# A fused attention and expert kernel: identity matmuls ahead of the first weights, x rows 2 and 3 loaded third, three jobs from VectorE to ScalarE

## The reference

```
xn = layernorm(x)                                   # over the 128 features
s  = attention(xn)          # blocks, top 64 tokens, windows of 32; gated; layernorm
q  = xn @ Wq.T              # 2 halves x 8 heads x 64
sim = einsum(q, keys)       # 32 keys for each half and head
sx, ix = top_k(sim[0], 16);  sy, iy = top_k(sim[1], 16)
scores, idx = top_k(sx[:, None] + sy[None, :], 16)
f  = sum over the 16 of  gelu(xn . W_down[idx]) * softmax(scores) * W_up[idx]
out = x + s * silu(f)
```

## Time and profile before

| what | value |
|---|---|
| runs of the kernel | 288.28, 289.41 and 291.24 us, median 289.41 us |
| profiled execution, span from first to last instruction | 288.0 us (no other time of this execution is given) |
| mean granted TensorE clock | 0.981 |
| busy share of the span: PE, DVE, ACT, POOL | 84%, 93%, 83%, 79% |
| chain that ended last: DVE, PE, issue, ACT, DMA | 77%, 8%, 6%, 4%, 2% |

### The profile page before, as it was taken

How to read it: one execution, slowest core, us unless ns; L and a number is a source line. 1 busy time by engine, 2 the same in 40 slices (tenths; PEclk the granted TensorE clock), 3 DMA queues, 4 the chain that set the end, 5 groups by cost and what they waited for, 6 DMA issues and landing times.

```text
span 288.0 us, 7869 instructions
## 1 busy us (share of the span) xinstructions
PE 241.3 (84%) x1504; PEld 170.5 (59%) x1504; DVE 267.8 (93%) x2574; ACT 238.1 (83%) x1071; POOL 228.8 (79%) x351
## 2 busy tenths in 40 slices
PE   0789997887989798979897989798979897988792
PEld 0624343474757675767575757575757575756592
DVE  6689999999999999999999999999999999997474
ACT  3338668589898999899989998999899989997832
POOL 8986710378688879997999799979997999798791
PEclk9999999799999999999999999999999999999959
DMA  8920000000000000100010001000100010001002
GB/s 173 272 67 1 3 1 0 0 3 0 2 3 0 2 3 0 39 3 1 1 41 0 3 1 38 5 0 2 38 2 2 3 36 2 5 0 38 3 1 71
DMA packets 11234, 6.27 MB, mean 22 GB/s; under 512 B 1457, under 2 KB 10674, under 8 KB 11186
## 3 DMA queue, kind: packets, MB, share of 16 engines
q1 hardware_dynamic: 9858, 5.12, 6.7%
q10 hardware_dynamic: 1328, 0.66, 1.2%
HBM read 3.67 MB, written 2.10 MB: 20 GB/s over the span
## 4 chain that ended last, share of the span: by engine, by line
DVE 77%; PE 8%; issue 6%; ACT 4%; DMA 2%; SPq 1%; DVEq 0%
DVE rest L1124 27%; DVE top L1113 15%; DVE top L1133 15%; DVE last L1157 7%; DVE slot_gap L1142 2%; DMA x_sb<-in_L_attn_hidden_states 2%; DVE sel_m L1176 2%; DVE st L1048 2%; PE scratch L1550 1%; ACT prob L808 1%; DVE slot_gap L1148 1%; DVE sel_b L1179 1%; DVE sel_a L1179 1%; PE c_bank L1523 1%; DVE mv L1052 1%
## 5 line engine op out<-in xcount | busy, mean ns | idle before, releaser
L1124 DVE MATCH_REPLACE8 rest<-top,sim 128x32 f32<-128x32 f32 x512 | 85.8, 180 | 0.0
L1133 DVE MAX8 top<-rest 128x8 f32<-128x32 f32 x512 | 53.5, 177 | 0.7
L808 ACT ACTIVATE prob<-drop 128x50 f32<-128x50 f32 x232 | 53.4, 255 | 0.0
L1113 DVE MAX8 top<-sim 128x8 f32<-128x32 f32 x496 | 51.1, 183 | 2.2 <-PE sim L1459 2.2
L808 ACT ACTIVATION_READ_ACCUMULATOR prob<-drop 128x1 f32 x232 | 48.7, 213 | 0.0
L488 POOL TENSOR_TENSOR squareT<-sideT 100x512 bf16<-100x512 bf16 x31 | 32.2, 1039 | 14.6 <-ACT sideT L723 14.6
L1124 DVE MATCH_VALUE_LOAD rest<-top,sim 128x8 f32 x512 | 41.1, 80 | 0.3
L1459 PE MATMUL sim<-sim_w,xT_all 128*128 128x512 f32 x64 | 35.2, 633 | 0.9 <-DVE sim_w L1090 0.9
L473 POOL TENSOR_TENSOR past<-gap,last 128x400 f32<-128x400 f32 x31 | 26.7, 862 | 11.4 <-DVE last L1157 11.3
L495 POOL TENSOR_TENSOR drop<-gap,out_by 128x400 f32<-128x400 f32 x31 | 32.0, 1033 | 2.8 <-ACT out_by L714 2.8
L1477 PE MATMUL t_bank<-gaps_of,topT 128*128 128x200 f32 x128 | 29.7, 354 | 2.4 <-ACT topT L728 2.3
(11 more groups left out here) (277 smaller groups left out, 720.0 us busy)
## 6 DMA issues: line engine op xcount, KB each, us to landing
out<-y_sb SPq DMA_DIRECT2D x7, 256.0 KB, 2.3
x_sb<-in_L_attn_hidden_states SPq DMA_DIRECT2D x2, 256.0 KB, 3.9
fwq_sb<-in_L_ffn_Wq ACTq DMA_DIRECT2D x2, 256.0 KB, 5.8
x_sb<-in_L_attn_hidden_states SPq DMA_DIRECT2D x1, 512.0 KB, 5.9
wc_sb<-in_L_attn_Wc SPq DMA_DIRECT2D x1, 256.0 KB
out<-last_y SPq DMA_DIRECT2D x2, 128.0 KB, 1.8
wo_in<-in_L_attn_Wo SPq DMA_DIRECT2D x1, 192.0 KB
keys_sb<-in_L_ffn_keys ACTq DMA_DIRECT2D x1, 128.0 KB, 3.4
```

Source lines behind the costliest of these rows:

```text
L808: last = nc.scalar.activation(prob[d][:, h, :], drop[:, h, :], ACT.Exp, scale=-1.0, accum_out=den[d][:, h:h + 1])
L1113: last = nc.vector.max(top[d][:, v, 0:8], sim_bank[d][:, bass.ts(v, KEYS)])
L1124: last = nc.vector.match_replace(out=rest[:, v, :], in_to_replace=top[d][:, v, 0:8], in_values=sim_bank[d][:, bass.ts(v, KEYS)], imm_value ...
L1133: last = nc.vector.max(top[n % 2][:, v, 8:16], rest[:, v, :])
```

## The change

ScalarE takes over the copy of the transposed keys (ahead of its expert selection copies), the normalisation of row 0 and the copy of the folded weights (both ahead of its loop over the rows). Rows 2 and 3 of x are loaded ahead of the six small loads. TensorE multiplies the identity by 112 of its own columns, 6 times ahead of the key transposes and 8 times behind them, into columns of a PSUM bank that nothing reads. GpSimd waits for row 0 ahead of normalising row 2, as both raise the same semaphore.

```diff
--- before.py
+++ after.py
@@ -298,8 +298,8 @@
         NORM_GROUPS = [(0, 1), (1, 2), (2, 4), (4, 6), (6, B)]
 
         POOL_NORMS = [1, 2, 4, 6]
-        ACT_NORMS = [3, 5, 7]
-        assert sorted([0] + POOL_NORMS + ACT_NORMS) == list(range(B))
+        ACT_NORMS = [0, 3, 5, 7]
+        assert sorted(POOL_NORMS + ACT_NORMS) == list(range(B))
 
 
 
@@ -338,12 +338,12 @@
 
             load_x(0)
             load_x(1)
+            load_x(2)
             sp.dma_start(zw_sb[:, 0:1], ws[:, :]).then_inc(zw_in, 16)
             sp.dma_start(zw_sb[:, 1:4], wg[:, :]).then_inc(zw_in, 16)
             for k, src in enumerate([bs[0:1], bg[0:1], bg[1:2], bg[2:3]]):
                 sp.dma_start(bz_sb[k * B:(k + 1) * B, :],
                              src.rearrange("(a n) -> a n", a=1).to_broadcast([B, 1])).then_inc(zw_in, 16)
-            load_x(2)
             load_x(3)
             for dst, src in ((down_sb, ffn_down), (wup_sb, ffn_up)):
                 sp.dma_start(dst[:, :, :], src[0:2 * P, :].rearrange("(k p) d -> p k d", p=P)).then_inc(down_in, 16)
@@ -447,6 +447,8 @@
                 pool.wait_ge(norm1_ready, g + 1)
                 for b in range(b0, b1):
                     if b in POOL_NORMS:
+                        if b == 2:
+                            pool.wait_ge(xn_done[0], 1)
                         for t in range(TB * b, TB * b + TB):
                             last = nc.gpsimd.tensor_scalar(xn_all[:, t, :], x_sb[:, t, :], rstd1[:, t:t + 1],
                                                            nmr1[:, t:t + 1], ALU.mult, ALU.add)
@@ -688,6 +690,13 @@
                                                 bias=nmr1[:, t:t + 1], scale=rstd1[:, t:t + 1])
                 last.then_inc(xn_done[b % 2], 1)
 
+            act.wait_ge(consts, 3)
+            act.wait_ge(keysT_ready, 1)
+            for half in range(2):
+                c = slice(half * DKEY, (half + 1) * DKEY)
+                last = nc.scalar.activation(keysT[c, :, half, :], f_bank[c, 0:HK].rearrange("p (h k) -> p h k", k=KEYS),
+                                            ACT.Copy)
+            last.then_inc(keysT_out, 1)
             act.wait_ge(consts, CONSTS)
             for at, length, i, j, di, dj in pair_runs(HALF_V):
                 chosen = bass.AP(ident, (i * TOPK + j) % P, [[P, P], [0, 2], [di * TOPK + dj, length]])
@@ -752,6 +761,9 @@
                     last = nc.scalar.activation(wo_sb[:, r, :], wo_in[:, r, :], ACT.Identity, bias=wo_mean[:, r:r + 1])
                 last.then_inc(wo_step, 1)
 
+            norm_rows(0)
+            act.wait_ge(fold_ready, 1)
+            nc.scalar.activation(sim_w[:, :], sim_bank[1][:, :], ACT.Copy).then_inc(sim_w_done, 1)
             for b in range(B):
                 act.wait_ge(xt_full, b + 1)
                 nc.scalar.activation(xT_all[:, bass.ts(b, L)], scratch[b % 2][:, :], ACT.Copy).then_inc(xt_out, 1)
@@ -1069,25 +1081,12 @@
             row_stats(0)
             dve.wait_ge(x_in[1], 16)
             row_stats(1)
-            dve.wait_ge(consts, 3)
-            dve.wait_ge(keysT_ready, 1)
-            for half in range(2):
-                c = slice(half * DKEY, (half + 1) * DKEY)
-                last = nc.vector.tensor_copy(keysT[c, :, half, :], f_bank[c, 0:HK].rearrange("p (h k) -> p h k", k=KEYS))
-            last.then_inc(keysT_out, 1)
-            dve.wait_ge(norm1_ready, 1)
-            for t in range(TB):
-                last = nc.vector.tensor_scalar(xn_all[:, t, :], x_sb[:, t, :], rstd1[:, t:t + 1],
-                                               nmr1[:, t:t + 1], ALU.mult, ALU.add)
-            last.then_inc(xn_done[0], 1)
             dve.wait_ge(gaps_step, 2)
             nc.vector.tensor_tensor(gaps_of[:, :, :], rank_first[:, :].unsqueeze(2).to_broadcast([P, HALF_H, CANDS]),
                                     rank_sum[:, :, :], ALU.subtract).then_inc(gaps_of_done, 1)
             dve.wait_ge(x_in[2], 16)
             row_stats(2)
             row_stats(3)
-            dve.wait_ge(fold_ready, 1)
-            nc.vector.tensor_copy(sim_w[:, :], sim_bank[1][:, :]).then_inc(sim_w_done, 1)
 
             def invert_sums(n):
 
@@ -1407,6 +1406,11 @@
         def _(pe):
             mm = nc.tensor.matmul
 
+            def keep_clock(count):
+
+                for _ in range(count):
+                    mm(t_bank[:, HEADS * CANDS:512], ident[:, :], ident[:, 0:512 - HEADS * CANDS], start=True, stop=True)
+
             def transpose_keys():
 
                 pe.wait_ge(keys_in, 16)
@@ -1738,7 +1742,9 @@
                 last.then_inc(gate_ready, 1)
 
             pe.wait_ge(consts, 2)
+            keep_clock(6)
             transpose_keys()
+            keep_clock(8)
             fold_weights()
             transpose_rows(0)
             pe.wait_ge(xt_out, 1)
```

## The result

The changed kernel took 292.24 us (median of 4 runs, 291.18 to 293.84) against 289.52 for the kernel before. The ratio is 1.0097, with a 95% interval of 1.0055 to 1.0138. A second comparison, with 12 runs, gave 291.95 against 288.87: 1.0090 (1.0057 to 1.0124). It is about 1% **slower**, and outside the range that I gave (287.2 to 291.0). The profiled execution took 291.63 us and has a span of 289.1 us, 1.1 above that of before. The ratios are taken over executions within 1.5% of the fastest of the same kernel, the medians over all.

A forecast was written before the change was run, and what follows sets the result against it. DVE, busy 93%, was taken to bound the kernel; of its 2.7 us lead 0.3 survives, so the span goes from 288.0 to 287.7 and, with the median 1.4 above it, the forecast is 289.1 us, range 287.2 to 291.0.

The forecast's parts named there:

- Where DVE's lead goes: At tile 0's pair gaps: of DVE's 2.7 us lead, 2.3 is waited away; the run gains 0.2 to 0.4 us.
- Step 4: Loads at the start: rows 2 and 3 of x, loaded third, delay the folded weights 0 to 2.9 us; 0.5 taken.
- Step 3: TensorE's start: 28 added identity passes delay the key transposes 0.35 us and end at 7.2 to 8.0 us if fast.
- the sum: Start to DVE's first MAX8 at the fast price: fold from 8.7, scores to 13.0 instead of 15.70, lead 2.7 us.
- Rival B: TensorE's start: lower clock, added passes delay the fold; MAX8 17.0, run 290.7, or 292.4 with fold at 11.1; chance 0.12.
- Rival C: On the path: one half-speed TensorE stretch more or less, 1.6 us, giving 287.5 or 290.7; chance 0.14.
- Steps 2 and 5: ScalarE takes DVE's three jobs, row 0 done at 10.0 us; GpSimd's added wait ahead of row 2; both cost nothing.
- second chain: GpSimd to 20.24 us, then TensorE and ScalarE to the first gap copy's end at 31.20, 0.4 us behind DVE.

## Why the prediction was wrong

**Where DVE's lead goes: right.** I said that a lead at MAX8 is waited away at the pair gaps, whose copy hangs on GpSimd's row 2, and that any MAX8 up to 15.3 us gives the same there. Pair gaps were taken at 31.08 both with MAX8 at 13.06 and at 14.93, with a wait of 2.0 us in the first case. The changed kernel never got there: its MAX8 started at 16.84 to 18.52.

**Step 4, the load order: mis-sized.** I took 0.5 us between bounds of 0 and 2.9. The fold came 2.3 to 2.9 us later in the four profiles, 2.7 with the load order alone: nearly the whole of the upper end. My reason for the lower end, that the small transfers had used the stretch anyway, was wrong. The six of them carry some 2 KB together; what they took was SyncE's time to issue them, from 1.82 to 4.39 us, and the load of x was issued only then, at 4.43. In the changed kernel its issue is the third of these and over by 2.32:

```profile
0.79 1.53 SPq L337 DMA_DIRECT2D x_sb<-in_L_attn_hidden_states  x3
```

So 512 KB entered while the weights, issued from 1.33 us on, were on their way. From 5 to 8 us the windows show 183 to 225 GB/s before and 187 to 286 after: the queues moved no less, and still the weights came later.

**Step 3 and the sum: the step that failed.** I set fold, transposes and scores at the fast price because the passes precede them, and let the passes end at 7.2 to 8.0 and the fold begin at 8.7. I did not ask what the clock does when TensorE has nothing to do between these. With the fold at 10.55 it fell, and the sum ended at 16.84 instead of 13.0. The late weights alone would have left MAX8 near 14.9, as in the profile with the clock held, within the 15.3 up to which I said that steps 3 and 4 need not be sized well. With the fall of the clock it went past that bound. Had I carried the upper bound of step 4 through, I would have seen a wait of over 3 us behind the passes. Nothing in the rows of before shows what follows such a wait: their fold was slow after 3.21 us, but TensorE had done only two passes until then and had not yet shown its faster pace.

**Rival B** forecast the right sign (290.7) and the late MAX8 (17.0), with a chance of 0.12. Its far end, the fold at 11.1 and 292.4 us, is close to the measured time and to the profile with the fold at 11.12. But its mechanism is another, so the agreement is luck: TensorE had reached the faster pace, and in the changed kernel's four profiles the passes were never in the fold's way; they ended at 6.9 to 7.9 us, 2.8 to 3.7 us ahead of it. The rule of the Trainium skill by which I discounted it (TensorE: Matmul & The Clock Gate, What's actually happening) also says that the clock goes back to half after idling. The trace agrees: work until 6.9, none until 10.5, and 1.2 GHz from 11.8. I used one half of the rule. Rival C named what happened, one more stretch at 0.50 on the path, but as scatter and not as something that the change brings about.

**Steps 2 and 5: right but for two times.** The three jobs alone cost the run next to nothing (1.0011), as said; the 0.35 us in DVE's middle no step had. ScalarE's table load moved behind the key transposes (from 2.73 to 5.18 us), so that the copies ended at 7.2, still ahead of the weights, and row 0 was normalised at 10.6 instead of 10.0. The late fold covered that. GpSimd's added wait shows nowhere, and its power over four columns took 1.05 us instead of 1.14 for row 1, with DVE's normalisation gone from beside it (1.14 also with the load order alone and with the passes alone, 1.04 with the jobs alone). The rule of the Trainium skill (GPSIMD Engine Reference, Specifications) agrees with that in sign, but by row 2 the chain had gained 0.04 us, not the 0.1 that I worked out from it.

**The accounts.** Of the 2.7 to 3.1 us, the profiles show 1.9 us (mean) to the first pair gaps, 0.35 in the middle, and 0.2 from there to the last tile's pair gaps (21.7 us with the jobs, 21.5 without). A further part lies outside the spans: the 18 recorded executions of the changed kernel are 1.7 to 2.7 us longer than their spans (mean 2.0), all those of before 1.7 to 1.8. What that is, the runs leave open. Where the 0.35 and 0.2 us come from was not tested.

## What to carry to other kernels

Work added to hold TensorE's clock has to last until the awaited data land. Here 28 passes that ended 3.7 us too early gave a faster start of the fold and half speed behind it, and passes up to the weights kept the full speed. But they have a price, since they are in the way where they outlast the data, as in the execution in which 48 of them took 8.06 us. Making TensorE early can even cost, because it then waits for another engine, and its clock can fall in that wait: with the load order undone this made the second chain 1.6 us late. Where a load is moved ahead, first find what it competes with on the other queue: here 512 KB of x delayed weights that were on the path, for rows that had time. And before counting a lead, follow the first input that does not move with it; here that limited the gain at the first pair gaps to some 0.5 us.

## What the runs showed of the hardware

In seven profiles a wait of TensorE in its first 20 us, 2.4 to 4.6 us long, came with a fall of the granted clock from 1.00 to 0.50: in the changed kernel (four profiles), with the load order undone, with the centring moved, and with the passes alone. In some the fall came within the wait (at 10.2 us in the two profiles of the changed kernel with the latest folds), in others after the work had begun again, in the changed kernel's first profile 1.2 us after. The clock then stayed at 0.50 for 3.5 to 10.2 us. The length of the wait alone does not tell: waits of 2.7 and 2.8 us for GpSimd's rows left the clock at 1.00 in two profiles (the kernel with GpSimd's constants moved, and the one with the clock held until the late weights), while 2.4 us with the passes alone and 2.8 us in one profile of the changed kernel came with the fall.

The time until TensorE reaches its faster pace also varies: the same 16 passes behind the key transposes took 2.0 us in two profiles of the changed kernel, 2.7 and 2.9 in the other two, and up to 3.3 in the kernels with the load order undone.

A load of 512 KB issued some 2.5 us earlier on SyncE's queue made 512 KB on ScalarE's queue land later: 7.1 us from issue to landing instead of 5.8, in the median of its two halves.
